# One floor per token instead of one clamp per tile, and the way-back factor on GpSimd, in a 1-core attention and feed-forward kernel

## The reference

```
def act_quant(x, bits=8):
    qb = float(2 ** (bits - 1))
    scale = qb / jnp.clip(jnp.max(jnp.abs(x), axis=-1, keepdims=True), EPS)
    xq = jnp.clip(jnp.round(x * scale), -qb, qb - 1) / scale
    return x + jax.lax.stop_gradient(xq - x)

def h_bitlinear(x, w):
    return jnp.einsum('bsh,oh->bso', act_quant(fwht(x)), weight_quant(w))

gate = bitlinear(x, w_gate)
up = bitlinear(x, w_up)
return h_bitlinear(jax.nn.silu(gate) * up, w_down)
```

## Time and profile before

| | |
|---|---|
| median of 3 runs | 398.62 us (398.0 to 398.7) |
| span of the profiled execution, first to last instruction | 396.3 us |
| mean granted TensorE clock in it | 0.926 |
| busy, share of the span | DVE 85%, ACT 80%, PE 76%, POOL 37% |

### The profile page before, as it was taken

The page is one execution under the profiler, slowest core; times in us unless marked ns, Lnnn a source line. Parts: engine busy times, 40 slices in busy tenths (PEclk is TensorE's granted clock), DMA queues, the critical chain, the costliest instruction groups (busy, mean ns, idle before and its releaser), DMA issues.

```text
span 396.3 us, 7494 instructions
## 1 busy us (share of the span) xinstructions
PE 301.0 (76%) x2589; PEld 186.2 (47%) x2589; DVE 338.2 (85%) x556; ACT 316.7 (80%) x517; POOL 144.8 (37%) x315
## 2 busy tenths in 40 slices
PE   7988999766796987567777857767576766884957
PEld 6755565322585874333444534444344343432434
DVE  4668999868889988778899998889999999678995
ACT  3785689967255789688999989899999999887771
POOL 6424524569500504004124565412222132247330
PEclk9989999899899999876899997999999999999576
DMA  8900023400200016569999988799899969800001
GB/s 268 388 5 3 0 74 96 203 2 0 106 0 2 2 29 124 107 99 173 163 168 175 177 158 132 140 185 174 151 156 166 156 130 148 136 1 2 26 31 50
DMA packets 126342, 42.68 MB, mean 108 GB/s; under 512 B 121056, under 2 KB 124768, under 8 KB 125536
## 3 DMA queue, kind: packets, MB, share of 16 engines
q1 hardware_dynamic: 125872, 41.60, 53.9%
q0 software_dynamic: 144, 0.52, 0.3%
q10 hardware_dynamic: 288, 0.07, 0.1%
HBM read 11.24 MB, written 1.05 MB: 31 GB/s over the span
## 4 chain that ended last, share of the span: by engine, by line
DVE 28%; PE 24%; ACT 23%; issue 16%; POOL 7%; DMA 1%; SPq 0%; ACTq 0%; DVEq 0%; POOLq 0%
ACT rb L973 15%; DVE nm L1452 5%; PE ps L1920 4%; PE ps L2015 4%; PE ps L1991 2%; DVE st L1108 2%; PE ps L2120 2%; PE ps L1785 1%; DVE ra L1557 1%; PE ps L2027 1%; DVE small L1559 1%; POOL ra L557 1%; POOL ra L558 1%; DMA xs<-x 1%; PE ps L1893 1%
## 5 line engine op out<-in xcount | busy, mean ns | idle before, releaser
L1452 DVE TENSOR_REDUCE nm<-ps 128x1 f32<-128x1024 f32 x128 | 153.1, 1217 | 12.6 <-PE ps L2015 11.6
L973 ACT ACTIVATE rb<-ps,eb,sq 128x1024 int16<-128x1024 f32 x128 | 153.7, 1214 | 11.8 <-POOL eb L639 11.1
L2015 PE MATMUL ps<-ra,rb 128*128 128x512 bf16 x256 | 82.8, 409 | 49.0 <-ACT rb L973 48.4
L639 POOL TENSOR_SCALAR eb<-nm,sq 128x1 f32<-128x1 f32 x128 | 34.2, 267 | 123.1 <-DVE nm L1452 122.1
L2015 PEld LDWEIGHTS ps<-ra,rb 128*128 128x128 bf16 x256 | 15.8, 99 | 67.7 <-ACT rb L973 63.9
L2042 PEld LDWEIGHTS ps<-ra,tern 128*128 128x128 f16 x624 | 26.0, 99 | 18.9 <-issue 9.2
L2042 PE MATMUL ps<-ra,tern 128*128 128x16 f16 x624 | 26.0, 171 | 2.6 <-DVE rb L1183 2.6
L973 ACT ACTIVATION_READ_ACCUMULATOR rb<-ps,eb,sq 128x1 f32 x128 | 27.0, 211 | 0.0
L1893 PE MATMUL ps<-xqT,tern 128*128 128x512 bf16 x64 | 17.2, 406 | 6.0 <-DVE rb L1361 4.9
L2027 PEld LDWEIGHTS ps<-idh,rb 128*128 128x128 f16 x224 | 14.3, 99 | 14.3 <-issue 7.7
L2027 PE MATMUL ps<-idh,rb 128*128 128x128 f16 x224 | 17.5, 222 | 4.6 <-issue 2.2
(11 more groups left out here) (240 smaller groups left out, 714.0 us busy)
## 6 DMA issues: line engine op xcount, KB each, us to landing
stage<-w SPq DMA_DIRECT2D x2, 1024.0 KB, 7.3
rb<-ra SPq DMA_DIRECT2D x16, 128.0 KB, 3.1
xs<-x SPq DMA_DIRECT2D x4, 256.0 KB, 4.5
cx<-ctx_in SPq DMA_DIRECT2D x4, 256.0 KB, 4.7
stage<-w_gate SPq DMA_DIRECT2D x1, 1024.0 KB, 7.7
stage<-w_up SPq DMA_DIRECT2D x1, 1024.0 KB, 10.6
stage<-w_down SPq DMA_DIRECT2D x1, 1024.0 KB, 4.8
cx<-wide_rows SPq DMA_DIRECT2D x1, 1024.0 KB, 7.9
```

Source lines behind the costliest of these rows:

```text
L639: nc.gpsimd.tensor_scalar(eb[:, u % 3:u % 3 + 1], nm[:, u % 3:u % 3 + 1], sq[:, t, h:h + 1], LN255, ALU.mult, ALU.add).then_inc(s_bias, 1)
L973: A(esc[u % E_RING], bank(2 * (u % 3), 2), ACT.Exp, bias=eb[:, u % 3:u % 3 + 1], scale=sq[:, t, h:h + 1], accum_out=es[:, t % 2, h:h + 1]) ...
L1452: V.tensor_reduce(nm[:, u % 3:u % 3 + 1], bank(2 * (u % 3), 2), AX.X, ALU.max, negate=True).then_inc(s_max, 1)
L2015: ins = M(bank(2 * (u % 3) + hf), qz[t % 2][:, h // 2, h % 2, :], kT[:, h // 2, 512 * hf:512 * hf + 512], start=True, stop=True)
```

## The change

`token_factors` gets two more operations on 128x8: a reciprocal of `fac`, and its product with EPS. That is `yfloor`, the clamp in the units of the rotated values. `y_scales` then has two column operations per tile after the maximum, where it had four: `ycl` is the larger of the maximum and `yfloor`, divided by 128, and `yqs` is its reciprocal. The factor for the way back, `ydq`, moves to GpSimd: `y_factors` makes `facw` once, and `y_factor(t)` multiplies `ycl` by it for each tile, after a wait for `y_scale`. `y_residual(t)` waits for a new semaphore `y_back` besides the one it had. `y_factor(4)` to `y_factor(7)` stand between the other steps of GpSimd's list.

```
-        fsum, fneg, fsq, fvar, frs, isd, ires, amr127 = (small[:, i, :] for i in range(10, 18))
+        fsum, fneg, fsq, fvar, frs, isd, ires, amr127, yfloor, facw = (small[:, i, :] for i in range(10, 20))
...
+            def y_factors():
+                pool.wait_ge(tok_fac, 1)
+                pool.wait_ge(w_scale, W1 + 1)
+                link(nc.gpsimd.tensor_scalar(facw, fac, wmean[:, DOWN:DOWN + 1], FP16_UNIT, ALU.mult, ALU.mult))
+
+            def y_factor(t):
+
+                pool.wait_ge(y_scale, t + 1)
+                c = slice(t, t + 1)
+                nc.gpsimd.tensor_scalar(ydq[:, c], ycl[:, c], facw[:, c], 1.0, ALU.mult, ALU.mult).then_inc(y_back, 1)
+
+            y_factors()
+            for t in range(4):
+                y_factor(t)
             x2_rstd_and_shift(0)
+            y_factor(4)
             x2_bp(0)
+            y_factor(5)
             x2_rstd_and_shift(1)
+            y_factor(6)
+            y_factor(7)
             x2_bp(1)
             x2_rstd_and_shift(2)
...
             def token_factors():
                 dve.wait_ge(w_scale, UP + 1)
-                V.tensor_scalar(fac, sd, wmean[:, UP:UP + 1], 1.0 / 32.0, ALU.mult, ALU.mult).then_inc(tok_fac, 1)
+                link(V.tensor_scalar(fac, sd, wmean[:, UP:UP + 1], 1.0 / 32.0, ALU.mult, ALU.mult))
+                link(V.reciprocal(yfloor, fac))
+                V.tensor_scalar(yfloor, yfloor, EPS, None, ALU.mult).then_inc(tok_fac, 1)
                 dve.wait_ge(tok_fac, 1)
...
                 link(V.tensor_reduce(ymx[:, c], bank(Y_BANK[t], 2), AX.X, ALU.max, apply_absolute_value=True))
-                link(V.tensor_scalar(ycl[:, c], ymx[:, c], fac[:, c], EPS, ALU.mult, ALU.max))
-                V.tensor_scalar(ydq[:, c], ycl[:, c], wmean[:, DOWN:DOWN + 1], FP16_UNIT / 128.0, ALU.mult, ALU.mult)
-                link(V.reciprocal(yrc[:, c], ycl[:, c]))
-                V.tensor_scalar(yqs[:, c], yrc[:, c], fac[:, c], 128.0, ALU.mult, ALU.mult).then_inc(y_scale, 1)
+                link(V.tensor_scalar(ycl[:, c], ymx[:, c], yfloor[:, c], 1.0 / 128.0, ALU.max, ALU.mult))
+                V.reciprocal(yqs[:, c], ycl[:, c]).then_inc(y_scale, 1)
 
             def y_residual(t):
                 dve.wait_ge(dn_ps, t + 1)
+                dve.wait_ge(y_back, t + 1)
```

More of the change, by code:

```diff
@@ L322, in build @@
         a_half = sem("a_half")
+        y_back = sem("y_back")
         tok_fac = sem("tok_fac")
```

## The result

The changed kernel took 397.61 us (median of 20 runs, 393.24 to 404.93), the kernel before 398.9 (20 runs, 396.94 to 401.7). The ratio is 0.993, 95% interval 0.9908 to 0.9952: faster by 1.9 to 3.7 us. The forecast was 398.9, with a range that ended at 397.7. The ratio leaves out the five runs of the changed kernel that lie more than 1.5% above its fastest, and none of the kernel before, whose runs spread less; over all 40 runs the medians stand 1.3 us apart and the means 0.9.

The account below looks back on a forecast made before the run. The chain was taken to run through token_factors and GpSimd's additions, then PE, then DVE from 119.68 to about 139 us. + 0.48 + 0 - 0.24 = + 0.24 us on 398.62 gave 398.9 us, range 397.7 to 399.6.

Parts of the forecast that it names:

- token_factors, + 0.48: Gate and up stage: the two added linked operations lie on the chain before gu_product(3) and cost 0.48 us.
- A tile, 1.95 to 1.57: Rotated stage, y_scales on DVE: from the maximum to the next instruction 1.57 us instead of 1.95, saving 0.38 a tile.
- about 1.1: Sign: DVE's idle time before down_correction in the rotated stage grows by about 1.1 us.
- No residual waited for `y_back`: Sign: y_back of a tile is there before its residual; a residual waiting for it would make the forecast wrong.
- So I take POOL as first: Tile 4: x2_bp(0) on POOL meets w_clip(4) and holds it, so the gain of tiles 3 to 5 becomes 0.
- the hold of 1.5 or more: Sign at tile 4: w_clip(4) takes 1.5 us or more rather than 0.69.
- rival A: w_clip(4) goes first and x2_bp(0) waits: - 0.93 + 0.48 = - 0.45, 398.2 us; chance 0.25.
- - 0.24 for `n_out(1)`: x2_bp(1) leaves q_quant4(0), which gets about 0.8 us shorter; PE saves its 0.24 us wait for n_out(1).
- Rival C: x2_bp(1) lands on q_quant4(1), which is on the path: + 0.24 + 0.8 = + 1.0, 399.7 us; chance 0.13.
- B: Rival: w_clip(4) first, and the gate and up stage takes up the 0.48: - 0.93, 397.7 us; chance 0.12 or 0.13.
- I expect it to carry the shift unchanged: Second attention: it repeats its pattern whatever its start, so the shift reaches the end unchanged.
- if the attention's length changes: Sign: a changed length of the second attention would make the forecast wrong; no size given.

Follow-up runs that it names:

- e1: Changed kernel with the two yfloor operations moved from token_factors to ahead of the first y_scales; 396.84 us, ratio to before 0.9915.
- e2: Changed kernel with x2_bp(0) put ahead of y_factor(4) on GpSimd, behind the same wait; 400.73 us, ratio to before 0.9979.
- e10: Changed kernel with the way-back factor made on VectorE and x2_bp waiting for no scale; 398.21 us in one run, before 398.74.
- e8: Kernel before with only x2_bp(1) made to wait for the scales of tile 7; 402.06 us in one run, before 401.68.
- the two cured kernels: Kernel before and changed kernel, each with 30 extra small matmuls ahead of q_project(2); 399.01 and 398.28 us.
- e5: Kernel before with 30 extra small matmuls in PE's pauses ahead of q_project(2); 399.01 us, ratio to before 0.9927.
- e11: Kernel of e1 with three 0.4 us memsets on GpSimd ahead of the layer norm's third factor; 400.69 us, ratio to before 1.0022.
- e12: Kernel of e1 with one 0.4 us memset on GpSimd ahead of the layer norm's third factor; 397.97 us, before 399.89.
- e4: Changed kernel run again with nothing edited; 397.67 us, before 399.82 on the same chip, ratio 0.9948.
- e13: Kernel of e1 run again, without memsets, beside e11 and e12; 394.86 us, before 399.89 on the same chip.
- e7: Kernel of e1 with 30 extra small matmuls ahead of q_project(2); 397.50 us, ratio to before 0.9894.

## Why the prediction was wrong, point by point

**token_factors, + 0.48.** Right: 0.43 to 0.45, on the chain; e1 took it away again.

**A tile, 1.95 to 1.57.** Right: 1.56 or 1.57 at tile 3 and 1.59 at tile 4, in every profile with the changed tiles and `y_factor` on GpSimd. For tiles 0 to 2 it was worth nothing, as said; VectorE's wait at `down_correction` grew from 0.42 to 1.18, by 0.76 and not by about 1.1, since the 0.38 of tile 0 already went into the wait for the second `hadamard`, ahead of the maximum of tile 1 (0.81 before, 1.19 after). No residual waited for `y_back`.

**"So I take POOL as first", the first step that failed.** The near tie was reckoned to the hundredth, and the hold of 1.5 or more was right for the side chosen (e2: 1.59). But in all eight profiles in which the two start within 0.01 of each other VectorE was undisturbed. I had settled it by a row in which VectorE, 0.04 ahead, was held; that was no evidence for this pair of operations. The eight are no rule either: in e10 `x2_bp(1)` meets another operation of VectorE to the hundredth, and VectorE is held. What settles a tie these rows do not show; in the changed kernel it fell to rival A's side. The Trainium skill (SBUF — State Buffer, "Who interferes with whom") says that issue order decides; no row here shows an order within 0.01, and e2 agrees once GpSimd is 0.23 ahead, while the earlier trace rows, by its printed starts, does not.

**- 0.24 for `n_out(1)`, mis-sized.** `x2_bp(1)` out of the way is worth 0.41 (e8), since PE's printed idle time began at a modelled end, 0.17 after the point from which the next group could have started. With the tiles, the rotated stage is 1.06 to 1.20 shorter at equal clock pattern; rival A had 0.93, which with 0.41 for 0.24 would be 1.10. Together with token_factors that is - 0.6 to - 0.8; the two cured kernels, 0.73 apart by their medians, are too noisy to confirm it.

**Rival C** did not come: `x2_bp(1)` at 145.89 stood beside `q_quant4(1)`'s first two operations, neither of which it held. Two chances of the forecast do not agree: B has 0.12 in one sentence and 0.13 in the next, so that the rest is 0.75 by the first.

**"I expect it to carry the shift unchanged", the second step that failed, and the larger one.** The attention began 1.1 to 1.2 earlier after the first `hadamard`, and at that start `q_project(2)` ran at a granted clock of 1.00 instead of 0.51: - 1.6 to - 1.7 on the chain. Both directions are shown: e5 removes the low stretch without moving the start, e11 and e12 move the start and bring it back, e2 does so by its 0.3. The sum by rows is + 0.44, less 1.06 to 1.20, less 1.65: 2.3 to 2.4 us less, within the interval of the ratio. It is a sum of single profiles: over all runs the two kernels are 0.9 (means) to 1.3 (medians) apart on the first chip, and 2.3 and 2.15 on e4's. The forecast named "if the attention's length changes" among what would make it wrong, but gave it no chance; it did not ask what a shift would do to the clock that the profile before shows at 156.8 us.

Among profiles of the long clock pattern without extra matmuls C is 3.36 up to B = 52.84 and 4.65 or more from 52.87 on. I would not trust that edge to the hundredth, since the low stretches themselves lie 0.8 apart against the first `hadamard`; and the two of the short pattern (before, e10) have a low stretch there at B = 51.6 and 51.7. Counted from the end of the low stretch at tile 4 the long pattern parts more widely: `q_project(2)` starts 26.1 to 26.5 us behind it where it ran at 1.00, and 26.8 to 27.4 where the clock fell. Nor is the low stretch one that stays in place and is missed by the matmuls: it began between 0.6 us ahead of their start and 0.5 behind it, while in the profiles without extra matmuls that kept the clock the next one came 7.6 to 8.0 us after their start.

The best kernel run is the changed one with the floor worked out late (e1 0.9915, e13 0.9872 with 0.9827 to 0.9917); extra matmuls on top of it (e7) kept to the same 0.99.

## What to carry to other kernels

Before a small gain is added up, mark on the trace where the granted clock is low and which matmuls on the chain lie there: a shift of 0.3 us was worth another 1.4 of C here, more than the edits themselves, and one execution's pattern is not another's. A near tie of two engines belongs in a forecast as two cases of equal chance, not as one settled by a distant row. And an idle time of PE that begins at a matmul's printed end can be less than the wait: here 0.24 for 0.41.

## What was not expected of the hardware

A GpSimd operation on one column took 4.35 us (`y_factor(1)` at 113.66; `y_factor(0)`, beside `w_clip(2)`, took 0.55, the other six 0.26 or 0.27). VectorE ran two long additions there; its timeline, 106 to 120 us:

```profile
113.48 2.27 DVE L1392 TENSOR_TENSOR rb<-rb 128x2048 f32<-128x2048 f32 x1
115.67 2.28 DVE L1394 TENSOR_TENSOR rb<-rb 128x2048 f32<-128x2048 f32 x1
117.87 1.22 DVE L1418 TENSOR_REDUCE small<-ps 128x1 f32<-128x1024 f32 x1
```

GpSimd ended at 118.01, with the second of them: it found no gap between the two. The same page and section of the Trainium skill says that a VectorE instruction with two SBUF inputs contends with a GpSimd one that reads SBUF; the row agrees, and shows that two such back to back count as one. It cost nothing here, since `y_residual(1)` came only at 127.42.
